# Second attention of a two-layer language tower in units: row maxima of one unit beside the columns of the last, stacks moved inside SBUF, causal select on GpSimd

## What is computed

```python
h = _rmsnorm(x, ln1_w)
q = (h @ wq.T)...; k = (h @ wk.T)...; v = (h @ wv.T)...
q = q * cos + _rotate_half(q) * sin
k = k * cos + _rotate_half(k) * sin
k = jnp.repeat(k, NREP, axis=1)          # NREP = 2
v = jnp.repeat(v, NREP, axis=1)
scores = jnp.einsum('bhtd,bhsd->bhts', q, k) / jnp.sqrt(jnp.float32(HD))
scores = jnp.where(causal[None, None], scores, jnp.float32(-1e+30))
att = jax.nn.softmax(scores, axis=-1)
y = jnp.einsum('bhts,bhsd->bhtd', att, v)...
x = x + y @ wo.T
```

## Time and profile before

| | |
|---|---|
| runs | 407.96, 406.57, 407.51 us; median 407.51 |
| profiled execution | span 405.0 us; its own device time isn't listed, and the median of the runs lies 2.5 us above the span |
| busy shares of the span | TensorE 80%, VectorE 64%, ScalarE 34%, GpSimd 19% |
| second attention, from the first projection to the last sum of squares | 65.5 to 192.2 us |

### The profile page before, as it was taken

How to read it: one execution, slowest core, us unless ns; L and a number is a source line. 1 busy time by engine, 2 the same in 40 slices (tenths; PEclk the granted TensorE clock), 3 DMA queues, 4 the chain that set the end, 5 groups by cost and what they waited for, 6 DMA issues and landing times.

```text
span 405.0 us, 4152 instructions
## 1 busy us (share of the span) xinstructions
PE 326.0 (80%) x1563; PEld 178.2 (44%) x1575; DVE 259.2 (64%) x428; ACT 139.5 (34%) x231; POOL 78.2 (19%) x77
## 2 busy tenths in 40 slices
PE   1358797505889999898999999999999972399994
PEld 0125563303224334335675545555545531156844
DVE  1497756855997673105778444555589999872485
ACT  2124344510003554884256333444446100012160
POOL 5780000000000000000000223121301888900000
PEclk9999999955856999999989999999999999689998
DMA  8651040099400000000000000000000000000001
GB/s 276 224 194 78 2 157 0 1 213 176 169 0 4 1 2 2 2 2 0 2 0 0 2 1 1 0 2 0 1 2 0 0 0 0 1 2 0 2 0 52
DMA packets 5411, 15.87 MB, mean 39 GB/s; under 512 B 1360, under 2 KB 1488, under 8 KB 4752
## 3 DMA queue, kind: packets, MB, share of 16 engines
q1 hardware_dynamic: 4880, 15.09, 12.7%
q0 software_dynamic: 512, 0.53, 0.6%
HBM read 13.86 MB, written 1.70 MB: 38 GB/s over the span
## 4 chain that ended last, share of the span: by engine, by line
PE 55%; DVE 25%; ACT 6%; POOL 6%; DMA 3%; issue 3%; SPq 2%; DVEq 0%; POOLq 0%
PE ps L247 53%; DVE rw L1163 7%; DVE share L1039 2%; POOL arena L357 2%; POOL arena L358 1%; DMA arena<-scr_k 1%; DVE arena L1330 1%; DVE arena L1240 1%; DVE arena L1331 1%; ACT arena L868 1%; POOL share L357 1%; DVE st L995 1%; POOL share L358 1%; DMA idt<-ident 1%; ACT L775 1%
## 5 line engine op out<-in xcount | busy, mean ns | idle before, releaser
L247 PE MATMUL ps<-arena 96*128 96x512 bf16 (+5 forms) x192 | 57.2, 377 | 24.0 <-DMA arena<-scr_k 18.0
L247 PE MATMUL ps<-bfc_s 128*128 128x512 bf16 (+1 forms) x262 | 63.0, 324 | 0.6 <-issue 0.4
L868 ACT ACTIVATE arena<-ps 128x1024 f32<-128x1024 f32 (+5 forms) x48 | 36.7, 811 | 64.9 <-PE ps L247 64.6
L1163 DVE TENSOR_REDUCE rw<-ps 128x1 f32<-128x512 f32 (+2 forms) x96 | 46.7, 549 | 17.0 <-PE ps L247 16.9
L247 PEld LDWEIGHTS ps<-arena 99*128 99x128 bf16 (+1 forms) x192 | 19.2, 104 | 60.7 <-DVE rw L1163 19.4
L247 PE MATMUL ps<-xs,e_hi 128*128 128x512 f32 x96 | 45.3, 472 | 0.4
L1240 DVE TENSOR_TENSOR arena<-ps,arena 128x512 f32<-128x512 f32 x48 | 33.1, 691 | 17.9 <-ACT arena L892 17.6
L892 ACT ACTIVATE arena<-ps 128x512 f32<-128x512 f32 x48 | 28.6, 597 | 43.2 <-PE ps L247 42.0
L337 POOL COPY xc<-arena 128x512 f32<-128x512 f32 x2 | 1.2, 610 | 197.0 <-DVE arena L1025 197.0
L247 PE MATMUL ps<-xs,e_lo 128*128 128x512 f32 x96 | 38.7, 403 | 0.0
L247 PEld LDWEIGHTS ps<-bfc_s 128*128 128x128 bf16 x269 | 28.3, 106 | 20.4 <-issue 4.9
(11 more groups left out here) (228 smaller groups left out, 488.6 us busy)
## 6 DMA issues: line engine op xcount, KB each, us to landing
w<-wpack SPq DMA_DIRECT2D x1, 2152.5 KB, 10.5
arena<-tm SPq DMA_DIRECT2D x2, 1024.0 KB, 5.7
arena<-epack SPq DMA_DIRECT2D x1, 1540.0 KB, 6.6
arena<-scr_q SPq DMA_DIRECT2D x12, 128.0 KB, 5.2
arena<-rope SPq DMA_DIRECT2D x1, 1024.0 KB, 12.9
tu_s<-tu SPq DMA_DIRECT2D x2, 512.0 KB, 7.6
tk_s<-tk SPq DMA_DIRECT2D x2, 512.0 KB, 9.2
scr_q<-arena SPq DMA_DIRECT2D x1, 768.0 KB, 3.6
```

Of the source, the lines that this page charges most:

```text
L247: return nc.tensor.matmul(o, l, r, start=start, stop=stop, **kw)
L868: nc.scalar.activation(dst, src, ACT.Exp, scale=HD ** -0.5).then_inc(S("exp_done"), 1)
L1163: V.tensor_reduce(dst, ps[:, row_bank(n), 0:wd], AXX, ALU.max).then_inc(S("max_read"), 1)
```

## The change

The attention is cut into units: (batch, half of the queries, pair of heads) for the columns (`COL_UNITS`, eight of them, 4 or 8 steps each, 48 steps in all), and six larger ones for the maxima (`TOP_UNITS`). A table `ORDER` is made when the program is built, and TensorE, VectorE and GpSimd all walk it. A step of columns is followed by up to two row items of a later unit. Three banks (`RING_BANKS`: 0, 1, 6) go round for row items, transposes of the maxima and everything of the end; bank 7 alone takes the weighted values; banks 2 to 5 take the columns.

Other parts: a row item may hold several heads, so that there are 78 reductions in place of 96, and they write the negated maximum. Pieces are written six to a partition, and 24 DMAs move them SBUF to SBUF into the stacks; the copies of the repeated pieces are made by ScalarE and GpSimd. GpSimd also splits the maxima in pieces, makes `e_lo`, and zeroes the masked part of the exponentials (`affine_select`) where TensorE added a mask to the columns. Two successive key tiles share the four column groups of `weighted`, and `y_transposes` adds the two halves with a matmul against `E("ii")`. `k` is laid on 128 partitions for the rotation, with tables of its own (`rope_k`). Layer 0's load of `e_raw` no longer waits for `gf`.

```diff
+TOP_UNITS = [(0, 0, (0, 1, 2, 3)), (0, 1, (0, 1)), (0, 1, (2, 3)), (1, 1, (0, 1)), (1, 1, (2, 3)), (1, 0, (0, 1, 2, 3))]
+COL_UNITS = [(0, 0, 0), (0, 0, 1), (0, 1, 0), (0, 1, 1), (1, 1, 0), (1, 1, 1), (1, 0, 0), (1, 0, 1)]
+TOP_OF = [0, 0, 1, 2, 3, 4, 5, 5]
+COL_STEPS = [(k, j) for k, (_, c, _) in enumerate(COL_UNITS) for j in range(4 * c + 4)]
+UNIT_END = [sum(4 * c + 4 for _, c, _ in COL_UNITS[:k + 1]) for k in range(len(COL_UNITS))]
+PT_SLOTS = 8
...
+for _m in range(len(TOP_UNITS)):
+    _items = [("rows", _m, _n) for _n in range(len(ROW_ITEMS[_m]))]
+    RING += _items[:2] + ([("top", _m - 1, 0)] if _m else []) + _items[2:]
+RING.append(("top", len(TOP_UNITS) - 1, 0))
+COLS_FROM = RING.index(("top", 0, 0)) + 7
+RING_BANKS = (0, 1, 6)
...
+for _s in range(len(COL_STEPS)):
+    ORDER.append(("cols", _s, 0))
+    if _s >= 4 and _s % 2 == 0:
+        ORDER.append(("pv", (_s - 4) // 2, 0))
+    for _ in range(min(len(_todo), ring_per_step(_s))):
+        ORDER.append(_todo.pop(0))
+    ORDER += y_items(_s)
+ORDER += [("pv", len(COL_STEPS) // 2 - 2, 0), ("pv", len(COL_STEPS) // 2 - 1, 0), ("y", 1, 0), ("yT", 0, 0), ("o", 0, 0)]
...
+                    sp.dma_start(qst[0:MROW, c, b * NH + hh],
+                                 pieces_q[c][at:at + 16].rearrange("p n t -> p (n t)")).then_inc(done, 16)
...
+            def top_pieces(m):
+                rows = 4 * len(TOP_UNITS[m][2])
+                x, pcs = mtop[m % 2][0:rows], mrow[0:rows, m % 2]
+                pool.wait_ge(S("ring_read"), RING_ORDER.index(("top", m, 0)) + 1)
...
+                step(nc.gpsimd.tensor_copy(pcs[:, 0], x))
+                step(nc.gpsimd.tensor_tensor(x, x, pcs[:, 0], ALU.subtract))
+                step(nc.gpsimd.tensor_copy(pcs[:, 1], x))
+                nc.gpsimd.tensor_tensor(pcs[:, 2], x, pcs[:, 1], ALU.subtract).then_inc(S("top_pieces"), 1)
...
+                nc.gpsimd.affine_select(out=v, in_=v, pattern=[[0, 2], [1, P + behind]], compare_op=ALU.is_ge, fill=0.0,
+                                        base=-behind, channel_multiplier=-1).then_inc(S("masked"), 1)
...
+            def weighted(pair):
...
+                if COL_STEPS[2 * pair][1] == 0 and k >= 1:
+                    pe.wait_ge(S("yT"), k)
...
+            def y_copy(k):
+                act.wait_ge(S("pv"), UNIT_END[k] // 2)
...
+                nc.scalar.copy(yT[:, k % 4], ps[:, 7]).then_inc(S("yT"), 1)
+            for n, (k, j) in enumerate(COL_STEPS):
+                act.wait_ge(S("cols"), n + 1)
...
+                nc.scalar.activation(pt[:, n % PT_SLOTS, :, lo:512], ps[:, bank:bank + 2, lo:512], ACT.Exp,
+                                     scale=HD ** -0.5).then_inc(S("exp_done"), 1)
+                if n - 4 in UNIT_END[:-1]:
+                    y_copy(UNIT_END.index(n - 4))
```

More of the change, by code:

```diff
@@ L97 @@
+ORDER += [("pv", len(COL_STEPS) // 2 - 2, 0), ("pv", len(COL_STEPS) // 2 - 1, 0), ("y", 1, 0), ("yT", 0, 0), ("o", 0, 0)]
+assert not _todo
+RING_ORDER = [x for x in ORDER if x[0] not in ("cols", "pv")]
 WCOLS = {}
@@ new lines, in score_rows @@
+            def score_rows(m, n):
+                b, c, _ = TOP_UNITS[m]
+                i, heads, key0, wd, part = ROW_ITEMS[m][n]
+                if n == 0 and m in (0, 1, 3, 5):
+                    group = (0, 1, 3, 5).index(m)
+                    pe.wait_ge(S("stacks%d" % group), (96, 96, 128, 64)[group])
+                bank = ring_bank()
+                for x, hh in enumerate(heads):
+                    ins = mm(ps[:, bank, x * wd:(x + 1) * wd], qst[0:MROW, c, b * NH + hh, i * P:(i + 1) * P],
+                             kst[0:MROW, b * NKV + hh // 2, key0:key0 + wd], start=x == 0, stop=part == 0)
+                if part == 1:
+                    o = ps[:, bank, 0:len(heads) * wd].rearrange("p (h t) -> p h t", t=wd)[:, :, wd - P:wd]
+                    ins = mm(o, ident_b, spread(mask_ts, 1, len(heads)), start=False, stop=True)
+                ins.then_inc(S("ring"), 1)
@@ new lines, in top_transpose, with score_cols @@
+            def top_transpose(m):
+                _, c, heads = TOP_UNITS[m]
+                if c == 0:
+                    pe.wait_ge(S("ring_read"), RING_ORDER.index(("rows", m, len(ROW_ITEMS[m]) - 1)) + 1)
+                else:
+                    pe.wait_ge(S("top_all"), m)
+                bank = ring_bank()
+                nc.tensor.transpose(ps[0:4 * len(heads), bank, 0:P], rw[:, m, 16:16 + 4 * len(heads)], idt[:]).then_inc(S("ring"), 1)
+            def score_cols(n):
+                k, j = COL_STEPS[n]
+                b, c, hp = COL_UNITS[k]
+                if n == 0:
+                    pe.wait_ge(S("af_done"), 2 * NK + 1)
+                if n >= 2:
@@ new lines, in out_projection @@
+            def out_projection(c):
+                pe.wait_ge(S("ring_read"), RING_ORDER.index(("yT", c, 0)) + 1)
+                bank = ring_bank()
+                for j in range(4):
+                    ins = mm(ps[:, bank, j * P:(j + 1) * P], xT[:, (4 * c + j) * P:(4 * c + j + 1) * P], W("wo2"))
+                ins.then_inc(S("ring"), 1)
+            for kind, x, y in ORDER:
+                if kind == "rows":
+                    score_rows(x, y)
+                elif kind == "top":
+                    top_transpose(x)
+                elif kind == "cols":
+                    score_cols(x)
+                elif kind == "pv":
+                    weighted(x)
+                elif kind == "y":
+                    y_transposes(x, y)
+                elif kind == "yT":
+                    token_transposes(x)
+                else:
+                    out_projection(x)
```

507 lines of the change are left out of this document (267 added, 240 removed).

## The result

The changed kernel takes 427.31 us (median of four runs, 422.24 to 428.69), beside 407.74 for the kernel before on the same chip. The ratio is 1.042 [1.034, 1.051]: slower. A repeat gave 424.63 (423.57 to 430.4) and 1.043 [1.035, 1.052]. Ratios compare undisturbed executions alone, so one can differ a little from the quotient of two medians. The sign was forecast; 427 lies outside the range of 400 to 425, and the point of 415.5 was 12 us too low; by the repeat it was 9, and the repeat's median would lie just inside the range. The profiled execution took 422.24 us with a span of 420.5, where the forecast said 413.1. It was the shortest of the four, and the part of the miss that lies in the other three can't be located.

A forecast was written before the change was run, and what follows sets the result against it. Second attention bound in turn by DRAM moves, VectorE's reductions, TensorE. First columns 98.5 + TensorE's work 52.5 + waits, clock, friction 32.8 = 183.8; end 16.5, to 200.3: span 413.1, plus 2.5 gives 415.5 us. Range 400 to 425.

The forecast's parts named there:

- term (3), the clock: TensorE comes out of the row stage at half clock; five us at half speed cost 2.5 us.
- Behind that nothing changes: After the second attention's last sum of squares, the rest of the kernel was forecast to take as long as before.
- Front: Up to VectorE's first reduction: it starts at 84.6 against 95.99, a gain of 11.4 us.
- My 418 by that rule: Forecast time had GpSimd's three copies and VectorE's operations excluded each other for whole instructions, adding 3.6 us, not 1.2.
- First columns: Start of the second attention's columns: 98.5 against 127.1, with 4.0 us for the maxima's DMAs and 0.8 for queued tables.
- Wait (1), bank 7: TensorE stands at the weighted values until ScalarE's exponential and copy are done: 1.95 us six times, 11.7 us.
- Wait (2), maxima: TensorE stands before columns while maxima are handed on, which takes 6.0 us: 3.6 + 3 x 3.0 + 1.0 = 13.6 us.
- rival that the maxima come in time: Sets of maxima are handed on before TensorE needs them, so 13.6 us of waits fall away: 402 us; chance 0.28.
- sign of being wrong: The change would be faster if maxima are handed on in under 4 us, or bank 7's copy is done before TensorE arrives.
- (4) friction: Three ring banks slow the steps: 12% of the 40 us with rows, 5.0 us.
- rival "the clock falls again": Stops put TensorE back at half clock in the four long units, 2 us lost in each: 423 us; chance 0.12.
- The end: From `y_transposes` of batch 1, half 1 to the last sum of squares: a chain of small steps, 16.5 us.

The follow-up runs named there:

- a2: The changed kernel with the tables tu and tk issued with the first loads, not ahead of the first maxima; 421.92 us, 1.030 of the kernel before.
- a1: The changed kernel with ScalarE copying bank 7 one exponential earlier; 413.65 us, 1.014 of the kernel before.
- a3: The changed kernel with eight more row items ahead of the first columns; 413.36 us, 1.011 of the kernel before.
- c2: The changed kernel with only two edits, bank 7 copied one exponential earlier and eight more row items ahead; 399.69 us, 0.977 of the kernel before.
- b1: The changed kernel with useless matmuls (four of 512 columns) at each of the end's waits; 419.67 us, 1.023 of the kernel before.
- b4: The changed kernel without GpSimd's selects and TensorE's waits for them, so the output is wrong; 426.65 us, 1.047 of the kernel before.

## Why the prediction missed

The sign and the mechanism were right: the front gains, the waits added take it back and more. The steps that failed are **term (3), the clock**, priced at 2.5 us in the middle and at nothing from the end on ("Behind that nothing changes"), and the **0.8 us** for small transfers queued behind the tables. In their place the runs showed three more stretches at half clock in the middle (5.5 us by an estimate below), 3.0 us more in the end and 3.2 behind it, and 4 to 5 us for the tables.

These are more than the 7.4 us by which the profiled execution missed, because other terms were too high: the waits for bank 7 by 1.6 us, those for the maxima by 4.8. That the sum came as near as it did is luck. The median lies 4.3 us further off. I had put it 2.5 us above the span; a run's time was 1.7 us above its span here, but the profiled execution was the shortest of four, and the median is 6.8 above its span. What made the others longer is not known.

Step by step:

- *Front.* 84.6 forecast, 83.95 measured. The company of GpSimd is in VectorE's and GpSimd's rows:

```profile
70.25 1.20 DVE L1300 TENSOR_TENSOR share<-share 128x512 f32<-128x512 f32 x1
...
75.47 1.19 DVE L1310 TENSOR_TENSOR arena<-tmp,arena 128x512 bf16<-128x512 f32 x1 [0.25 <-ACT arena L988]
```

```profile
69.88 1.03 POOL L400 COPY arena<-arena 128x1024 bf16<-128x1024 bf16 x1 [39.84 <-ACT arena L988]
74.55 1.56 POOL L400 COPY arena<-arena 128x1024 bf16<-128x1024 bf16 x1 [3.64 <-ACT arena L988]
```

  Two operations of 0.69 took 1.20 and 1.19: 1.0 us, where I said 1.2. Less 0.69, the first would have begun at 70.76, about when the copy ends (70.91), and GpSimd's second copy took 1.56 instead of 1.03 beside an operation of VectorE's that began at 74.52. By the Trainium skill (SBUF — State Buffer, "Who interferes with whom") the one waits until the other is done, and these rows agree better with that than with both running slower. My 418 by that rule was wrong in its sum, not in the rule: it let all three copies stop VectorE for their whole length, and only the tails of two did (for some 0.5 us each).
- *First columns.* 98.5 forecast, 101.13 measured. The four GpSimd operations took 1.6 us (1.4 forecast). Then 8.0 us pass up to the first columns, where I had 4.0 and 0.8. Missing were SP's own queue, which is free 1.6 us after the pieces are done (94.70 against 93.14), and 5.08 us for a transfer that takes 1.70 with the tables out of its way (a2). I had counted when the tables' bytes are through, 97.3, as if the small ones shared the queues up to then.
- *Wait (1), bank 7.* 11.7 forecast, 10.1 in TensorE's rows. Right in kind, 1.6 too high. a1 removes 7.2 of the page's 10.8 and gains 11, the rest of it with the clock.
- *Wait (2), maxima.* 13.6 forecast for the sets behind the first, 16.0 - 7.2 = 8.8 on the page. Handing on takes 5.4 us, not 6.0, and TensorE gets to the wait later, since it is slower than I said. a3 shortens the wait by 12.6 and gains 13. The rival that the maxima come in time, to which I gave 0.28, didn't happen, and its 402 was wrong as well: a3 has them in time behind the first set and takes 413.4, 1.1% above the kernel before. My sign of being wrong ("if the maxima are handed on in under 4 us, or if the copy of bank 7 is done before TensorE gets there") says "or" where it takes both: a1 and a3 alone stay 1.4 and 1.1% above the kernel before, and c2 has both and takes 399.7.
- *(3) Clock and (4) friction.* Of the 83.9 us from the first columns to the `y_transposes`, 52.5 (own work), 10.1 and 8.8 leave 12.5 for these two; I had 7.5. The clock was not low once but in four stretches there, which give the rows above their 0.56 (101 to 107), 0.51 (113 to 120) and 0.76 (171 to 185, two of them). Read in slices of half a us it is at 0.50 up to 106.2, from 113.2 to 119.9, from 171.1 to 174.5 and from 181.4 to 184.8, with TensorE busy for 5.1, 4.5, 3.2 and 3.4 us. Half of this, 8.1 us, is an estimate of what it cost. The first stretch, 2.6, is the one that I had priced at 2.5; the other three, 5.5, stand nowhere in my sum. The 4.4 left are the friction, where I said 5.0. The rival "the clock falls again", with 0.12, partly came true. For that case I said 423, and 424.6 to 427.3 was measured. The Trainium skill (TensorE: Matmul & The Clock Gate, "HAM oscillation — how this bites in real kernels") tells of loops whose waits throttle the array again and again; the trace agrees, with 0.51 from 113 to 120 behind the waits for the second set, and I gave it too small a chance against its own evidence.
- *The end.* 16.5 forecast, 19.5 measured: counted with prices at full clock, on a chain with many waits (its terms add up to 16.65, too). With useless matmuls in the waits (b1) it is 4.0 us shorter, which makes 15.5.
- *Behind.* Forecast unchanged, measured 3.2 longer. The end hands on a TensorE at 0.50, so that the cover matmuls took 8.61 us, 1.3 more. The expert matmuls behind them then run at 0.50 for longer than before: the clock is 0.66 from 214.5 to 224.5, where the same ten us had 0.83 before (202.2 to 212.2), some 1.7 us of work. With b1, 213.1 behind the last sum of squares and 0.83.
- *Selects.* Hidden, as forecast (b4).

What stays open: why the clock falls behind some stops and not others (of the three waits of 1.9 to 2.1 us for maxima none did it, of the six copies of 1.7 two), what the clock in the middle is worth as an experiment, since no run held it there with the waits in place, and what makes the changed kernel's times spread from 422 to 428 beyond the clock.

## What to carry over

Price an added wait twice: the stop itself, and the half clock of the work behind it, and follow that to the next place where TensorE is the bound; here filling the stops gave back 7 us, and the rows of one execution put the second part at more, beside 19 us of waits. When several engines hand a small result round, give the producer a lead of more work items rather than shorten the relay: one number in the order table (a3) gained as much as any other single edit, and a consumer's buffer should be copied out when it is full, not one step later. Small urgent transfers must not be issued behind megabytes that nobody needs yet.

## What the runs showed of the hardware

A transfer of 4 KB in the queues behind 2 MB took 5.08 us, and 1.70 with the tables loaded earlier (a2). The 24 moves of 96 KB from SBUF to SBUF landed in 2.8 us (median) and cost SP 0.63 us of issuing each (8 issues in 5.09 us). The time to landing stayed between 2.7 and 3.0 us over all 24, so SP's issuing set their pace, though with the DMA engines busy for 0.86 to 0.90 (80 to 95) there was little room left. GpSimd's `affine_select` took 0.41 us for 128x256 and 0.62 for 128x512 elements. With matmuls without use in the waits of the end, some 0.9 us at a time, it took 13.5 us from its first drain in each of five executions, and 14.9 to 18.9 in ten without them.
